# Per-slot input columns of a routed MLP: copied by GpSimd from register addresses, instead of gathered by matmuls on TensorE

## The reference, cut to what matters

```python
rw = softmax(cond_8)                      # (128 rows, 8 experts)
w, sel = top_k(rw, 2)                     # two experts for each row
w = w / w.sum(-1)
out = sum over the two experts e of a row:
          w_e * ( gelu(x1 @ gate[e]) * (x1 @ up[e]) ) @ down[e]      # 128 -> 512 -> 128
out = out + ( gelu(x1 @ shared_gate) * (x1 @ shared_up) ) @ shared_down
```

## Time and profile before

| | us |
|---|---|
| three runs: lowest, median, highest | 522.19, 524.23, 526.32 |
| the profiled execution, its own time | 522.42 |
| its span, first to last instruction | 520.7 |

### The profile page before, as it was taken

How to read it: one execution, slowest core, us unless ns; L and a number is a source line. 1 busy time by engine, 2 the same in 40 slices (tenths; PEclk the granted TensorE clock), 3 DMA queues, 4 the chain that set the end, 5 groups by cost and what they waited for, 6 DMA issues and landing times. The chain is left out here.

```text
span 520.7 us, 7597 instructions
## 1 busy us (share of the span) xinstructions
PE 412.3 (79%) x2740; PEld 366.4 (70%) x2740; DVE 347.5 (67%) x579; ACT 286.3 (55%) x423; POOL 148.8 (29%) x139
## 2 busy tenths in 40 slices
PE   2868768699999999999999989999968791000097
PEld 2657536699999999999999977777745570000097
DVE  2565337598897777767777754666536688989733
ACT  1445566365645555545545446556636588929370
POOL 1365750130000000000000014676424106977140
PEclk9997867899999999999999999999969996555589
DMA  8188865175667656676676135000000000000012
GB/s 262 64 288 258 282 209 237 42 262 194 203 253 248 218 191 252 200 268 229 228 265 236 68 102 242 1 1 0 1 0 0 1 0 0 1 1 0 0 62 102
DMA packets 31205, 71.22 MB, mean 137 GB/s; under 512 B 3904, under 2 KB 20032, under 8 KB 25920
## 3 DMA queue, kind: packets, MB, share of 16 engines
q1 hardware_dynamic: 28976, 66.33, 36.7%
q0 software_dynamic: 288, 4.19, 2.0%
q10 hardware_dynamic: 1904, 0.20, 0.3%
HBM read 55.12 MB, written 15.60 MB: 136 GB/s over the span
## 5 line engine op out<-in xcount | busy, mean ns | idle before, releaser
L183 ACT ACTIVATE Gb<-ps 128x512 f32<-128x512 f32 x110 | 65.9, 599 | 102.5 <-PE ps L177 101.6
L177 PE MATMUL ps<-xgh,Wr 128*128 128x256 f32 x624 | 116.9, 288 | 2.2 <-DVE xgl L186 2.2
L177 PEld LDWEIGHTS ps<-xgh,Wr 128*128 128x128 f32 x624 | 97.5, 193 | 2.4 <-issue 2.4
L177 PE MATMUL ps<-xgl,Wr 128*128 128x256 f32 x312 | 88.6, 284 | 0.0
L186 DVE TENSOR_TENSOR Hf<-Gb,ps 128x512 f32<-128x512 f32 x78 | 53.5, 687 | 43.4 <-PE ps L177 43.1
L669 PE MATMUL ps<-WD,Hh 128*128 x312 | 75.8, 333 | 0.0
L672 PE MATMUL ps<-WD,Hl 128*128 x312 | 69.4, 222 | 0.0
L177 PEld LDWEIGHTS ps<-xgl,Wr 128*128 128x128 f32 x312 | 60.1, 192 | 0.0
L672 PEld LDWEIGHTS ps<-WD,Hl 128*128 128x128 f32 x312 | 59.8, 192 | 0.0
L741 POOL DMA_INDIRECT G<-yscr,sidx x2 | 2.2, 1076 | 199.0 <-ACT HSh L183 198.7
L669 PEld LDWEIGHTS ps<-WD,Hh 128*128 128x128 f32 x312 | 58.9, 189 | 0.0
(11 more groups left out here) (184 smaller groups left out, 885.8 us busy)
## 6 DMA issues: line engine op xcount, KB each, us to landing
Wr<-wscr SPq DMA_DIRECT2D x39, 1024.0 KB, 4.8
wscr<-wst SPq DMA_DIRECT2D x16, 512.0 KB, 3.4
yscr<-Yb SPq DMA_DIRECT2D x39, 128.0 KB, 2.0
stg<-n_L_cond_skill_gate_dram SPq DMA_DIRECT2D x8, 256.0 KB, 4.7
stg<-in_L_cond_skill_up_dram SPq DMA_DIRECT2D x8, 256.0 KB, 4.2
stg<-n_L_cond_skill_down_dram SPq DMA_DIRECT2D x8, 256.0 KB, 5.3
out_dram<-X SPq DMA_DIRECT2D x7, 256.0 KB, 2.0
X<-in_x_dram SPq DMA_DIRECT2D x3, 512.0 KB, 6.1
```

What stands on the lines that cost most here:

```text
L177: return lambda e: e.matmul(o_, l, r, start=start, stop=stop, skip_group_check=True)
L183: return lambda e: e.activation(o_, i_, func, **kw)
```

## The change

`X1` is turned once, in stage 2, for all 32 steps and all rows (`turn_x` in place of `early`: four transposes, then ACT and DVE on 128x512), and its halves are kept in `XT` (channels x half x t x row, 32 KB per partition). `route` also multiplies the row numbers with `Pm`, on TensorE, so that `ordI` holds for each slot the number of its row as an integer. `fetch(i)` then fills the tile's place in the ring `xg` of `XR = 4`: for each of its 8 slots POOL loads the row number into a register and copies the slot's 32 + 32 columns (both halves, a step of 128 elements between one t and the next) from `XT`. `unit` waits for the last of the 8 copies; `fetch(i + 4)` waits for the units of tile i. All `gather` calls go, in the loop and in the shared stage, which reads `XT` itself. Three more `yield`s in `route` move its later pieces by three places. The splitting of the shared weights stands behind `fetch(0)` to `fetch(3)` on POOL.

```diff
...
-CH = 13
+XR = 4
...
-        Pm = at("Pm", [128, NSLOT], F32)
+        ordI = at("ordI", [1, NSLOT], I32)
-        XW = CH * SL * T
-        xg0 = [at("xgh0", [128, XW], F32R), at("xgl0", [128, XW], F32R)]
+        XT = at("XT", [128, 2, T, 128], F32R)
...
+        Pm = at("Pm", [128, NSLOT], F32)
+        bcI = at("bcI", [128, 1], I32)
+        bcF = at("bcF", [128, 1], F32)
...
-        xg1 = [at("xgh1", [128, XW], F32R), at("xgl1", [128, XW], F32R)]
-        xg = [[xg0[p], xg1[p]] for p in range(2)]
+        xg = at("xg", [128, XR, 2, SL * T], F32R)
...
+        k_bc = pool.do(lambda e: e.iota(bcI[:, :], pattern=[[0, 1]], base=0, channel_multiplier=1))
...
             yield
-            tok["P"] = dve.do(stt(Pm[:, :], iof[:, :], S[:, 43:44], tmpP[:, :], ALU.is_equal, ADD), (dve.sem, dve.n))
+            dve.do(cp(bcF[:, :], bcI[:, :]), k_bc)
+            d_ = dve.do(stt(Pm[:, :], iof[:, :], S[:, 43:44], tmpP[:, :], ALU.is_equal, ADD), (dve.sem, dve.n - 1))
+            yield
+            yield
+            p_ = pe.do(mm(bank[6][0:1, 0:NSLOT], bcF[:, :], Pm[:, :], True, True), d_)
+            yield
+            tok["ord"] = dve.do(cp(ordI[:, :], bank[6][0:1, 0:NSLOT]), p_)
             yield
 
...
-        got = {("m", 0): []}
...
-        def places(A, t0, nt):
-            return A[:, :].rearrange("p (s t) -> p t s", t=T)[:, t0:t0 + nt, :]
-
-        WS = SL * CH
-
-        def early(j):
+        d_xt = []
+
+        def turn_x(j):
 
             B = bank[4 + j % 4]
             for t in range(4):
-                p_ = pe.do(mm(B[:, WS * t:WS * t + WS], X1[:, 4 * j + t, :], Pm[:, 0:WS], True, True),
-                           d_q[j], *fbx[4 + j % 4], *lastA, d_P, sig=(t == 3))
-            src = B[:, 0:4 * WS].rearrange("p (t s) -> p t s", s=WS)
-            hi, lo = (places(xg[p][0], 4 * j, 4) for p in range(2))
-            a = act.do(acp(hi, src), p_)
-            d_ = dve.do(tt(lo, src, hi.bitcast(F32), SUB), a)
+                p_ = pe.do(tr(B[:, 128 * t:128 * t + 128], X1[:, 4 * j + t, :], identF[:, :]),
+                           d_q[j], *fbx[4 + j % 4], *lastA, sig=(t == 3))
+            hi, lo = (XT[:, a, 4 * j:4 * j + 4, :].rearrange("p t b -> p (t b)") for a in range(2))
+            a = act.do(acp(hi, B), p_)
+            d_ = dve.do(tt(lo, B, hi.bitcast(F32), SUB), a)
             fbx[4 + j % 4] = (d_,)
-            got[("m", 0)] += [a, d_]
+            d_xt.append(d_)
 
...
-                early(j - 3)
+                turn_x(j - 3)
         part1 = [(pool.sem, pool.n), (dve.sem, dve.n), (act.sem, act.n), (pe.sem, pe.n)]
...
-        s_sh = [sem(f"s_sh{k}") for k in range(2)]
-        k_s = {}
...
-        fxg = [(), ()]
...
-        nx = 0
-
-        units = {("m", c): list(range(0, T, 4)) for c in range(1, 3)}
-        units.update({("s", j): [4 * j] for j in range(8)})
-
-        def gather(key, both=True):
-
-            nonlocal nx
-            kind, c = key
-            t0 = units[key].pop(0)
-            k = nx % 2 if both else 0
-            nx += 1
-            B = BX[k]
-            half = c % 2 if kind == "m" else 1 - c // 4
-            w = WS if kind == "m" else 128
-            for t in range(4):
-                o_, i_ = B[:, w * t:w * t + w], X1[:, t0 + t, :]
-                f = mm(o_, i_, Pm[:, WS * c:WS * c + WS], True, True) if kind == "m" else tr(o_, i_, identF[:, :])
-                p_ = pe.do(f, *first, *fX[k], d_P, sig=(t == 3))
-            src = B[:, 0:4 * w].rearrange("p (t s) -> p t s", s=w)
-            if kind == "m":
-                hi, lo = (places(xg[p][half], t0, 4) for p in range(2))
-            else:
-                hi, lo = (xg[p][half][:, 512 * (c % 4):512 * (c % 4) + 512].rearrange("p (t s) -> p t s", s=128) for p in range(2))
-            a = act.do(acp(hi, src), p_, *first, *fxg[half])
-            d_ = dve.do(tt(lo, src, hi.bitcast(F32), SUB), a)
-            fX[k] = (d_,)
-            got.setdefault(key, []).extend([a, d_])
+        regb, k_xg = {}, {}
+
+        def fetch(i):
+
+            for s in range(SL):
+                def ld(e, s=s):
+                    regb[s] = e.value_load(ordI[0:1, SL * i + s:SL * i + s + 1], min_val=0, max_val=127)
+                pool.items.append(((d_ord,), ld, None, 0))
+                k_xg[i] = pool.do(lambda e, s=s: e.tensor_copy(
+                    xg[:, i % XR, :, T * s:T * s + T], XT[:, :, :, bass.ds(regb[s], 1)].rearrange("p a t o -> p a (t o)")),
+                    *d_xt, *first, *opt(p_unit, i - XR), sig=(s == SL - 1))
 
         def unit(i, u):
 
-            c, k = i // CH, i % CH
-            xs = slice(SL * T * k, SL * T * k + SL * T)
-            xh, xl = (xg[p][c % 2][:, xs] for p in range(2))
-            pe.wait(*got[("m", c)], l_wr[i], k_wm, a_wm, *fG[u], *fU[u], *first)
+            xh, xl = (xg[:, i % XR, a, :] for a in range(2))
+            pe.wait(k_xg[i], l_wr[i], k_wm, a_wm, *fG[u], *fU[u], *first)
             for m, B in ((0, BG[u]), (1, BU[u])):
...
-            if i + 1 == NT or k == CH - 1:
-                fxg[c % 2] = (p_,)
...
         def shared_up(n):
 
             j, q, b = n // 4, n % 4, n % 2
-            xs = slice(512 * (j % 4), 512 * (j % 4) + 512)
-            xh, xl = (xg[p][1 - j // 4][:, xs] for p in range(2))
+            xh, xl = (XT[:, a, 4 * j:4 * j + 4, :].rearrange("p t b -> p (t b)") for a in range(2))
             ws = slice(128 * q, 128 * q + 128)
             for m, B in ((0, BG[b]), (1, BU[b])):
-                pe.do(mm(B, SHh[m][:, ws], xh, True, False), *got[("s", j)], k_sh, *(fG[b], fU[b])[m], sig=False)
+                pe.do(mm(B, SHh[m][:, ws], xh, True, False), k_sh, *(fG[b], fU[b])[m], sig=False)
...
         p_down = {}
+        for i in range(XR):
+            fetch(i)
+        s_sh = [sem(f"s_sh{k}") for k in range(2)]
+        k_s = {}
+        for m in range(3):
+            dst, src = stgB[:, m % 2, :], (hg, hu, hd)[m]
+            if m == 2:
+                dst, src = dst.rearrange("p (c h) -> p c h", c=4), src.rearrange("(c p) h -> p c h", p=128)
+            l = sp.dma(lambda e, dst=dst, src=src: e.dma_start(dst, src), s_sh[m % 2], m // 2 + 1, *part1, *opt(k_s, m - 2))
+            hi, lo = (SHh[m][:, :], SHl[m][:, :]) if m < 2 else (SD[:, 0, :], SD[:, 1, :])
+            a = pool.do(ts(hi, stgB[:, m % 2, :], 1.0, 0.0, MUL, ADD), l, *part1)
+            k_s[m] = pool.do(tt(lo, stgB[:, m % 2, :], hi.bitcast(F32), SUB), a)
+        k_sh = k_s[2]
...
                 if i + 3 < NT:
                     load_tile(i + 3)
+                if i + XR < NT:
+                    fetch(i + XR)
             else:
...
-            nxt = ("m", i // CH + 1)
-            if nxt[1] < 3:
-                if units[nxt]:
-                    gather(nxt)
-            elif i < NT:
-                for j in range(4):
-                    if units[("s", j)]:
-                        gather(("s", j))
-                        break
...
-            if n < 16 and units[("s", 4 + n // 4)]:
-                gather(("s", 4 + n // 4), False)
```

More of the change, by code:

```diff
@@ L466, in program @@
         a_wm = (act.sem, act.n)
-        d_w01, d_sidx, d_P, d_et = tok["w01"], tok["sidx"], tok["P"], tok["et"]
+        d_w01, d_sidx, d_ord, d_et = tok["w01"], tok["sidx"], tok["ord"], tok["et"]
         d_ = dve.do(red(S[:, 180:181], S[:, 184:192], ALU.max), *d_red.values())
```

## The result

The changed kernel takes 541.95 us (median of 4 runs, 541.11 to 543.89), the one before 524.12 (4 runs). The ratio is 1.0344, 95% interval 1.0294 to 1.0394: slower by 3.4%, 18 us. The forecast was 562 (540 to 610). The direction and the engine that sets the loop were right, and the time lies at the low edge of the range; the size was not right, 18 us instead of 40.

What follows compares the result with a forecast made beforehand. TensorE bounded the loop before; GpSimd's slots at 0.74 us would bound it after. Profiled 522.4 us, plus 41.2 for tile 38's later start, minus 1.5 in the shared stage, gave 562 us, range 540 to 610.

Steps and rivals of the forecast that it cites:

- What bounds the loop: Expert loop: bound by TensorE before, by GpSimd's chain of slots after; tiles follow in 5.9 us instead of 4.73.
- a slot at 0.74 us: Expert loop on GpSimd: load, register operations, assertion and address 0.483 us plus five gaps of 0.05; 5.92 us a tile.
- turning point of 0.61: Slot time in us at which GpSimd's chain over 312 slots would end as before; below it the kernel gets faster.
- Stage 2 and head: Before the loop: shorter DVE subtractions save 2.0 us, routing costs 0.5; stage 2 ends at 97.4 instead of 98.87.
- The splitting in the chain: Six operations on the shared weights, on GpSimd behind the first four fetches: 7.1 us added to the chain.
- The copy at nothing: Each slot's copy on GpSimd takes 0.24 us, hidden under the next slot's 0.74 us of register work.
- The load on GpSimd: Register load in each slot, with no earlier row on GpSimd; taken from SP's 0.271 us and TensorE's 0.302.
- Faster: Rival: GpSimd keeps pace at 0.52 us a slot, loop stays bound by TensorE, kernel takes 509; keeps pace or nearly 0.11.
- No overlap: Rival in the loop: load waits for the copy before it, 0.98 us a slot, 637 us; chance 0.08 together with slow copy.
- slow loads: Rival in the loop: each load costs 0.54 us instead of 0.27, 84 us more, 646; chance 0.04.
- a fallen clock: Rival in the loop: granted clock below 0.9; chance 0.02.
- The tail: Shared stage behind the loop: four gathers go, 0.38 us each, so 1.5 us shorter.

## Why the prediction was right and wrong, point by point

**What bounds the loop: right.** The loop went from TensorE's clock to GpSimd's sequencer. One load instead of eight gives TensorE the loop back at 4.72 us a tile, and neither the ring nor the weights of tile 3 move the end.

**The step that failed: a slot at 0.74 us.** The chain has 311 distances between copies. From the first copy at 94.49 to the last at 314.79 it is 220.3 us; less the 6.35 us that the splitting adds, 213.9 / 311 = 0.688. The forecast's 0.74 is 0.052 more, 16 of the 20.3 us by which tile 38 was expected too late (335.4 against 315.1). The durations were read rightly: 0.483 forecast, 0.494 measured. The 0.01 added towards TensorE's sequencer (0.76, for its longer load) was right too: GpSimd's load took 0.287, not SP's 0.271. The gaps were wrong, by two errors of the same sign. The working took the median durations, 0.849 together, from a distance of 1.14 us; the three issues make only two intervals, and the instructions in these took 0.897 and 0.877, which leaves gaps of 0.25 and 0.26, 0.043 each and not 0.05. And GpSimd's gaps are shorter still than SP's: 0.03 each, and 0.07 for the copy's issue and the next load together, 0.17 us in all instead of 0.25.

A slot's price is therefore 0.66 when nothing disturbs it, 0.08 below the forecast. The mean is 0.688, which is 8.7 us in all, mostly by two disturbances that the forecast did not have (last section). It is by this luck that the time lies within the range: 541.95 - 8.7 = 533 would have been below its end of 540. At the turning point of 0.61 the result hung on less than a tenth of a microsecond, and an error of 7% in a duration that occurs 312 times became one of half the effect.

**Stage 2 and head: too dear by 2.9 us.** The chain was to start at 97.4, with the end of stage 2; stage 2 ended at 93.6 and the first copy came at 94.5, so 0.9 us between the two, at nothing in the forecast, hid part of the error. The forecast took DVE's shorter operations as the gain (2.0 us) and left out that ACT and DVE wait for TensorE there: the gain was 3.5 to 4.5. The 0.5 us for the routing cannot be read from the head of a single execution, whose start of stage 2 spreads from 77.5 to 79.2 in the nine kernels. With the third staging buffer the start was 1.7 us late, and the kernel took 2 us longer.

**The splitting in the chain: near enough**, 7.1 forecast, 6.35 measured (7.01 between two copies instead of 0.66). That the third load on SP holds up tile 3's weights came as forecast, though by 9 us and not 8, at no cost, as two runs show.

**The copy at nothing: right**, with 0.29 us instead of 0.24; the doubled copies show that it is covered: in an undisturbed slot a second one costs its issue, 0.04 us. The 0.24 was an estimate from two contiguous operations; copies back to back do start 0.24 apart. The copy's step of 512 bytes was varied in no run, so what share of its 0.29 us the step has is not shown.

**The load on GpSimd: near the rows of the other engines.** It took 0.287 us in the median, between SP's 0.271 and TensorE's 0.302, and 0.714 at most; eight numbers together took 0.565.

**The rivals.** Faster: it did not come, but the slot was 0.08 from it, and with one load a tile the changed kernel is on its side, 505.7 against the 509 worked out. The half clock at the start, in that working, is one the kernel before shows: 0.50 granted from 99.3 to 102.0 us. No overlap and slow loads fell, and so did a fallen clock, which has 0.02 of the chances; the granted clock was 1.00 from 180 to 220 us, with TensorE busy for 90% of the time instead of the 80% forecast.

**The tail: right as far as it can be told**, 1.5 forecast, 1.8 measured. From the start of tile 38 to the end it is 224.6 to 224.9 us in six of the seven kernels that make no gathers there and 226.2 in the seventh (the identity matmuls), against 226.5 and 227.9 in the two that make them. The spread within a kind is as large as the effect.

## What to carry to other kernels

Work moved to an idle engine is not free work: count what its sequencer executes, register loads and address arithmetic included, which the busy share does not show (here 0.66 us a slot, of which it shows the copy's 0.29), and divide by the time that the bound engine leaves. Where one small price occurs hundreds of times, name the slot time at which the sign turns and ask what could take the sum below it; here, reading eight registers with one load, with the register operations and assertions that fell away with it, turned 3.4% lost into 3.4% gained. And a pause that the bounding engine does not share costs nothing: shifting it or making it 20 us long left the distance from the first copy to tile 38 at 220 us.

## What the runs showed that was not expected

- Register loads do not cost in proportion: 0.287 us for one number, 0.317 for four neighbouring ones, 0.565 for eight.
- Once in 128 instructions (127 to 129 apart) GpSimd's sequencer paused for 0.29 us more, 12 times in the loop of the changed kernel, 3.5 us in all, and 12 times with the third staging buffer. The timeline shows one such distance, 0.96 instead of 0.66, while the load at 221.5 took its usual 287 ns:

```profile
221.48 0.29 POOL L594 CAST xg<-XT 128x64 fp32r x1 [0.36 <-issue]
222.44 0.29 POOL L594 CAST xg<-XT 128x64 fp32r x1 [0.66 <-issue]
```

- In 22 of the 312 slots the load took 0.33 to 0.69 us instead of 0.287, 4.3 us in all. In each of them the last transfer that SP had issued was a result write to HBM (`yscr`), in 20 of the 22 by 0.7 to 1.1 us before; of the 23 loads that started 0.65 to 1.1 us behind such a write, 20 were slow, and of the other 288 in the loop 2. The write ahead of one of the longest (0.677 us), in SP's timeline:

```profile
215.67 0.38 SPq L651 DMA_DIRECT2D yscr<-Yb  x1
```

and that load, in the per-line view of GpSimd's sequencer:

```profile
L592 POOLq TENSOR_LOAD <-ordI x1: 677/677/677, 216.4 to 216.4; - x1
```

That the write delays the load is only argued from this coincidence; no run took the writes away. Both effects together, 7.8 us, are most of the 8.7 us by which the mean slot, 0.688, exceeds 0.660.
- Of the 312 copies of the changed kernel, 27 took 0.6 to 1.4 us instead of 0.29, and 25 of the 27 ran beside DVE's subtraction `Hl`, which reads two operands from SBUF; of the 214 copies that did not run beside it, 2 were so long. With the copies doubled 71 were so long, and 68 of these ran beside `Hl`. In GpSimd's timeline two such copies take 1.62 us:

```profile
207.81 1.62 POOL L594 CAST xg<-XT 128x64 fp32r x2 [0.37 <-issue]
```

and in DVE's the two subtractions at the same time:

```profile
207.81 1.47 DVE L187 TENSOR_TENSOR Hl<-Hf,Hh 128x512 fp32r<-128x512 f32 x2
```

That one slows the other is only argued; no run parts them. Such a copy is longer than the 0.66 us of register work that covers it. The copies behind it start less than 0.66 apart (0.44 us at 209.4), so the chain catches up, and the two effects above leave at most 0.9 of the 8.7 us to it.
